# Attention block over 32 batches: projections in f16 parts, probability transposes laid between products, adj copied by ScalarE

## The reference

```python
h = jnp.maximum(_layernorm(x, axis=-1), 0.0)
q = split_heads(h @ Wq.T); k = split_heads(h @ Wk.T); v = split_heads(h @ Wv.T)
a = jnp.einsum('bhnd,bhmd->bhnm', q, k) * scale + (adj + adj)[:, None]
p = softmax of a over the last axis, 0 for a row of a that is all zero
o = einsum('bhnm,bhmd->bhnd', p, v), heads side by side
out = x + o @ Wo.T
```

## Time and profile before

| | us |
|---|---|
| median of 3 runs | 1319.92 (1319.8 to 1320.41) |
| the profiled execution | 1319.87 |
| its span | 1318.1 |
| PE busy | 1288.6 (98% of the span) |
| PE weight loads | 1225.6 (93%) |
| DVE busy | 1130.4 (86%) |
| ACT busy | 1033.8 (78%) |
| POOL busy | 902.1 (68%) |

### The profile page before, as it was taken

One profiled execution on the slowest core, in us unless ns is written; L12 is line 12 of the kernel. 1 busy time (PEld: TensorE's weight loads), 2 busy tenths in 40 slices (PEclk: granted clock), 3 DMA queues, 4 the chain that ended last, 5 costly groups with the idle time before them and its releaser, 6 DMA issues. The chain is left out here.

```text
span 1318.1 us, 43774 instructions
## 1 busy us (share of the span) xinstructions
PE 1288.6 (98%) x13072; PEld 1225.6 (93%) x13072; DVE 1130.4 (86%) x4023; ACT 1033.8 (78%) x2379; POOL 902.1 (68%) x1263
## 2 busy tenths in 40 slices
PE   5899999999999999999999999999999999999996
PEld 5899999999999999999999999999999999999995
DVE  5888888888888888888889888888888888888884
ACT  3788778788787888887888787888788887788874
POOL 5667667667677676676776676776677776676765
PEclk9999999999999999999999999999999999999998
DMA  6445454455354454454454454454544554544441
GB/s 213 104 117 138 108 136 119 115 139 127 109 146 117 109 148 119 112 143 116 114 151 109 122 130 121 123 143 108 131 119 122 133 133 110 139 119 113 126 121 49
DMA packets 90772, 163.88 MB, mean 124 GB/s; under 512 B 14976, under 2 KB 23168, under 8 KB 90752
## 3 DMA queue, kind: packets, MB, share of 16 engines
q1 hardware_dynamic: 90752, 163.64, 47.9%
HBM read 46.14 MB, written 16.78 MB: 48 GB/s over the span
## 5 line engine op out<-in xcount | busy, mean ns | idle before, releaser
L849 POOL TENSOR_TENSOR fold<-minus 128x512 f32<-128x512 f32 x256 | 329.7, 1288 | 325.3 <-DVE bounds L703 325.3
L553 ACT ACTIVATE probs<-minus,bounds 128x256 f32<-128x256 f32 x1024 | 460.2, 500 | 19.1 <-DVE bounds L703 19.1
L564 ACT ACTIVATE pT_hi<-pT_ps 128x512 f16<-128x512 f32 x512 | 306.0, 598 | 154.3 <-PE pT_ps L401 152.6
L721 DVE TENSOR_TENSOR pT_lo<-pT_ps,pT_hi 128x512 f16<-128x512 f32 x512 | 351.1, 686 | 84.5 <-ACT pT_hi L564 84.2
L703 DVE CUSTOM_DVE_ANT_0 minus<-s_ps,adj_now 128x256 f32<-128x256 f32 x1024 | 389.3, 417 | 18.3 <-DVE adj_now L715 14.3
L401 PE MATMUL pT_ps<-ident,probs 128*128 128x128 f32 x2048 | 307.6, 273 | 1.7 <-ACT probs L553 1.6
L328 PE MATMUL job_ps<-hT_hi,w_hi 128*128 128x256 f32 x1024 | 300.4, 293 | 3.1 <-DVE hT_lo L671 2.6
L328 PE MATMUL job_ps<-hT_lo,w_hi 128*128 128x256 f32 x1024 | 290.1, 283 | 0.0
L328 PE MATMUL job_ps<-hT_hi,w_lo 128*128 128x256 f32 x1024 | 289.8, 283 | 0.0
L401 PEld LDWEIGHTS pT_ps<-ident,probs 128*128 128x128 f32 x2048 | 240.4, 140 | 15.4 <-ACT probs L553 2.6
L390 PE MATMUL s_ps<-qk_stack 96*128 96x256 f32 x1024 | 247.1, 323 | 2.2 <-DMA qk_stack<-qk_parts 2.2
(11 more groups left out here) (80 smaller groups left out, 2406.4 us busy)
## 6 DMA issues: line engine op xcount, KB each, us to landing
qk_stack<-qk_parts SPq DMA_DIRECT2D x768, 128.0 KB, 2.3
x_in<-x SPq DMA_DIRECT2D x32, 512.0 KB, 3.4
x_res<-x SPq DMA_DIRECT2D x32, 512.0 KB, 3.6
out<-y SPq DMA_DIRECT2D x64, 256.0 KB, 2.1
adj_in<-adj SPq DMA_DIRECT2D x32, 256.0 KB, 3.6
minus<-wq_t SPq DMA_DIRECT2D x2, 512.0 KB, 6.0
qk_parts<-wv SPq DMA_DIRECT2D x2, 512.0 KB, 10.5
y<-wk_t SPq DMA_DIRECT2D x1, 512.0 KB, 8.4
```

The lines of the kernel that those rows point to most:

```text
L553: end = nc.scalar.activation(probs[hh % 2][:, t, :], minus[hh // 2 % 2][:, hh % 2, t, :], ACT.Exp, bias=bounds[:, hh // 2 % 4, 2 * (hh % 2 ...
L564: nc.scalar.activation(pT_hi[hh % 4][:, :, :], pT_ps[hh % 2][:, :].rearrange("p (m n) -> p m n", m=NT), ACT.Copy).then_inc(pT_high, 1)
L721: nc.vector.tensor_tensor(pT_lo[hh % 4][:, :, :], pT_ps[hh % 2][:, :].rearrange("p (m n) -> p m n", m=NT), pT_hi[hh % 4][:, :, :], ALU.sub ...
L849: nc.gpsimd.tensor_tensor(f1[:, :, :], src[:, :, 0:N // 2], src[:, :, N // 2:N], ALU.add).then_inc(folded1, 1)
```

## The change

Query, key and value products take f16 operands. The three weights come in untransposed, each half is scaled per row by a power of two so that its largest value is near 2^14, transposed on PE, and split in f16; the normalised tokens are multiplied by 2^9. The scales are taken out where the results are read (`q_scale`, `UNTOP`). The output projection stays in float32r.

On PE the units of the step's jobs are laid between the transposes and the scores: T, unit, T, unit, T, unit, T, unit, S, unit, S, unit, then the rest of the units, and V last (before: T, S, V, units). A transpose job now counts 4 units. h1 stands at the start of step 5, ahead of the second half of y0, and is taken at the end of step 5 rather than in step 6. The copy of adj goes from DVE (step 14) to ACT (step 13).

```diff
-PRODUCTS = {"qk": 24, "v": 12, "y": 12, "h": 1, "o": 1}
+PRODUCTS = {"qk": 24, "v": 12, "y": 12, "h": 4, "o": 4}
 JOBS = {
...
-    3: [("v", 3, 0, 3, 12), ("o", 1, -1, 0, 1)],
-    4: [("h", 0, 1, 0, 1), ("y", 0, -1, 0, 6)],
-    5: [("y", 0, -1, 6, 9), ("h", 1, 1, 0, 1), ("y", 0, -1, 9, 12)],
+    3: [("v", 3, 0, 3, 12), ("o", 1, -1, 0, 4)],
+    4: [("h", 0, 1, 0, 4), ("y", 0, -1, 0, 6)],
+    5: [("h", 1, 1, 0, 4), ("y", 0, -1, 6, 12)],
...
+TAKEN_AT_ONCE = ("h", 1)
...
-        w_hi = [sb(f"w_hi{i}", [P, KT, D], F32R) for i in range(4)]
-        w_lo = [sb(f"w_lo{i}", [P, KT, D], F32R) for i in range(4)]
-        WQ, WK, WV, WO = range(4)
+        WQ, WK, WV = range(3)
+        w_hi = [sb(f"w_hi{i}", [P, KT, D], F16) for i in range(3)]
+        w_lo = [sb(f"w_lo{i}", [P, KT, D], F16) for i in range(3)]
+        wo_hi, wo_lo = sb("wo_hi", [P, KT, D], F32R), sb("wo_lo", [P, KT, D], F32R)
...
-        hT_hi = sb("hT_hi", [P, KT, N], F32R)
-        hT_lo = sb("hT_lo", [P, KT, N], F32R)
+        hT_hi = sb("hT_hi", [P, KT, N], F16)
+        hT_lo = sb("hT_lo", [P, KT, N], F16)
...
+            def work(b, hh, first, last, start, stop):
+
+                at = 0
+                for kind, n, d, here, end in jobs_at(hh, first, last):
+                    lo, hi = max(here, here + start - at), min(end, here + stop - at)
+                    if lo < hi:
+                        job(kind, n, d, lo, hi, b)
+                    at += end - here
...
             def body(b, first, last):
                 for hh in range(HEADS):
-                    transpose_probs(b, hh, first and hh < 2)
-                    if hh + AHEAD < HEADS:
-                        scores(b, hh + AHEAD)
-                    elif not last:
-                        scores(b + 1, hh + AHEAD - HEADS)
+                    done = 0
+                    for m in range(NT):
+                        for t in range(NT):
+                            transpose_probs(b, hh, m, t, first and hh < 2)
+                            work(b, hh, first, last, done, done + 1)
+                            done += 1
+                    for t in range(NT):
+                        if hh + AHEAD < HEADS:
+                            scores(b, hh + AHEAD, t)
+                        elif not last:
+                            scores(b + 1, hh + AHEAD - HEADS, t)
+                        work(b, hh, first, last, done, done + 1)
+                        done += 1
+                    work(b, hh, first, last, done, 1000)
 
                     for was in range(hh - 2, hh) if hh % 2 == 0 else ():
                         if was >= 0:
                             values(b, was, first and was < 2)
                         elif not first:
                             values(b - 1, HEADS + was, False)
-                    for kind, n, d, start, stop in jobs_at(hh, first, last):
-                        job(kind, n, d, start, stop, b)
...
                     for kind, n, d in ended_before(hh, first, last):
                         take(kind, n, b + d, first and (kind, d) in (("v", 0), ("qk", 0)))
+                    if hh == HEADS - 3 and not last:
+                        copy_adj(b + 1)
                     high_probs(b, hh, first and hh < 4)
+                    for kind, n, d in ended_in(hh, first, last):
+                        take(kind, n, b + d)
...
+                nc.vector.tensor_reduce(w_scale[:, i, EXTENT, part], w_in[i][:, part, :], AX_X, ALU.max,
+                                        apply_absolute_value=True).then_inc(w_extent, 1)
...
-                        if hh + 2 == HEADS:
-                            copy_adj(b + 1)
                         shift(b + 1, hh + 2 - HEADS, False)
```

More of the change, by code:

```diff
@@ L210, in settled, with weight_waits @@
             engine.sem_inc(went_on[name], 1)
[L212 to L217, removed]
+        def weight_waits(engine, i, half):
+            engine.wait_ge(w_split, TURNS.index((i, half)) + 1)
         def bank(kind, n, b):
@@ L338, in job @@
                 if kind == "h":
-                    if n == 0:
+                    if n == 0 and start == 0:
                         pe.wait_ge(h_ready, b + (d + 1))
[L342 to L345, removed]
+                    for k, t in [divmod(i, NT) for i in range(start, stop)]:
+                        end = nc.tensor.transpose(ps[:, k * N + t * P:k * N + (t + 1) * P],
+                                                  h[:, t, (2 * n + k) * P:(2 * n + k + 1) * P], ident[:, :])
                 elif kind == "qk":
+                    half = PRODUCTS["qk"] // 2
                     if n == 0 and start == 0:
+                        pe.wait_ge(taken["h"], count("h", 0, b + d))
+                    if n == 0 and start <= half // 2 < stop:
                         pe.wait_ge(taken["h"], count("h", 1, b + d))
-                    half = PRODUCTS["qk"] // 2
                     for i, w in enumerate((WQ, WK)):
@@ L361, in job @@
                 elif kind == "o":
[L363 to L367, removed]
+                    if start == 0:
+                        pe.wait_ge(o_ready, (b + d) * PAIRS + 4 * (n + 1))
+                    for k, t in [divmod(i, NT) for i in range(start, stop)]:
+                        end = nc.tensor.transpose(ps[:, k * N + t * P:k * N + (t + 1) * P],
+                                                  o[:, t, (2 * n + k) * P:(2 * n + k + 1) * P], ident[:, :])
                 else:
@@ L482, in _ @@
                 values(B - 1, hh, False)
[L483 removed]
+            job("o", 1, -1, 0, 4, B)
             for n in range(NT):
@@ L647, in low_weight @@
[L647 to L660 removed]
+                at = 3 * TURNS.index((i, half))
@@ new lines, in low_weight @@
+            def low_weight(i, half):
+                at = TURNS.index((i, half))
+                dve.wait_ge(w_high, at + 1)
+                for j in range(2):
+                    cols = slice(half * HALF, (half + 1) * HALF)
+                    end = nc.vector.tensor_tensor(
+                        w_lo[i][:, 2 * j:2 * j + 2, cols],
+                        turn_ps[at % 3][j][:, :].rearrange("p (k n) -> p k n", k=2),
+                        w_hi[i][:, 2 * j:2 * j + 2, cols], ALU.subtract)
```

331 lines of the change are left out of this document (178 added, 153 removed), and 2 rows, old and new, of the table JOBS.

## The result

The changed kernel takes 1550.67 us (median of 4 runs, 1548.86 to 1551.16) against 1319.86 for the kernel before; the ratio is 1.1747, with a 95% interval of 1.1726 to 1.1767. It is slower, as forecast, but by 84 us more than the forecast of 1466 and above the range, which ended at 1530.

A forecast was written before the change was run, and what follows sets the result against it. PE was taken to bound the kernel at 39.8 us a batch. New PE work 35.2, waits 8.5 and clock 0.8 make 44.5 a batch; with 5 us ahead of the loop, 1466 us, range 1390 to 1530.

The forecast's parts named there:

- PE work: PE's products, transposes, S and V in a batch of the new order, without waits: 35.2 us, 4.6 less than 39.8.
- v0 behind y1: Step 14: PE waits 1.2 us for v0's bank, since y1 is taken 3.7 after V of step 12.
- v3 behind qk3: Step 2: PE reaches v3 before DVE, busy in its own order, has taken qk3, and waits 1.7 us.
- o1 behind v2: Step 4: o1 waits 0.7 us for v2, which DVE ends 2.2 us after the V of step 2.
- h0 behind v3: Step 4: h0 waits 1.3 us for v3, which DVE ends about 3.95 us after the V of step 2.
- h1 behind h0: Step 5: h1's bank is free 2.65 us after V, with one T between; PE waits 2.5 us.
- qk0 behind y0: Step 6: y0 ends with step 5 and ACT has other work ahead of it; PE waits 0.8 us.
- qk3 behind v0: Step 0: PE waits 0.3 us at qk3 behind v0.
- clock: Behind the new pauses, some products of y0 and qk0 run at half clock in some batches: 0.8 us a batch.
- the price of T between products: 42 T laid beside f16 products hide their f32 weight load and cost 0.055 us each instead of 0.108.
- Rival 2: Waits come, overlap doesn't: T stays 0.108, f16 products 0.12; 1526 us with the clock, 1500 without; chance 0.14.
- Rival 3: ACT and DVE take earlier jobs in time, so DVE sets the pace: 36.5 us a batch, 1226 us; chance 0.09.

The follow-up runs named there:

- t_f16: The changed kernel with probabilities, identity and the result of T as f16, so the low part of the probabilities is lost; 1468.92 us.
- fast kernel: The changed kernel with PE's order of before and h1 back at its old place, keeping f16 products, scales and adj's copy on ScalarE; 1286.65 us.
- order_f32r: The kernel before with the changed kernel's order on PE, places of taking and adj copy on ScalarE, products still float32r; 1563.10 us.
- grouped_v_last: The changed kernel without the alternation: four T, two S, all units, then V, with h1 at the start of step 5; 1465.32 us.
- v_early: The changed kernel with V right behind the unit after the second S, ahead of the rest of the units; 1435.45 us.
- h1_back: The changed kernel with h1 alone back behind three products of y0 and taken in step 6; 1488.18 us.
- f16_old_adj_dve: The kernel with f16 products and the order of before, with the copy of adj back on DVE ahead of the shift; 1286.92 us.

## Why the prediction failed, step by step

| us a batch | predicted | measured |
|---|---|---|
| PE work | 35.2 | 38.5 |
| v0 behind y1 | 1.2 | 1.1 |
| v3 behind qk3 | 1.7 | 1.4 |
| o1 behind v2 | 0.7 | 0.5 |
| h0 behind v3 | 1.3 | 1.2 |
| h1 behind h0 | 2.5 | 2.5 |
| qk0 behind y0 | 0.8 | 0.8 |
| qk3 behind v0 | 0.3 | 0 |
| waits in all | 8.5 | 7.5 |
| clock | 0.8 | 1.1 |
| batch | 44.5 | 47.05 |

The measured waits are from start to start (h1: 620.82 - 618.18, less the usual 0.11), as means over the batches at full clock; the idle times of the waits view are some 0.2 shorter each, since they begin where a matmul's length ends. The work is 45.98 less the waits.

- **The step that failed is the price of T between products,** the term 42 x 0.055 in the new PE work of 35.2. "I read the 0.108 as the loading of f32 weights" was wrong, and with it 0.055 for such a T: laid between products it cost 0.109, as among transposes. t_f16 puts that price on the 128 f32 data columns. 42 T x 0.054 = 2.3 of the 3.3 that the work was sized too low.
- **With T in f16** a batch at full clock is 43.65, less 8.3 of waits 35.35. That this is about the 35.2 of the sum is chance in part: t_f16 halves all 64 T where the sum halved 42, which is 1.2 less work, and the sum lacks what lies between kinds of work, about as much.
- **The trace of before had a sign of it,** in the mean lengths of its lines view by shape (busy us, mean ns), below. A product of 256 columns is 283 ns long and one of 65 is 192, so one of 128 would be near 222 by an estimate in a straight line between them; T with its 128 f32 columns is 273, and the f16 T of t_f16 is 223. The profile models where a matmul ends, so this is a sign and no proof.

```profile
L401 PE MATMUL pT_ps<-ident,probs 128*128 128x128 f32 x2048 | 307.6, 273 | 1.7 <-ACT probs L553 1.6
L328 PE MATMUL job_ps<-hT_lo,w_hi 128*128 128x256 f32 x1024 | 290.1, 283 | 0.0
L422 PE MATMUL o_ps<-v_parts,pT_hi 128*128 128x65 f16 x2048 | 153.6, 192 | 1.4 <-DVE pT_lo L721 1.0 <-issue 0.2
```

- **The rest of that term is what lies between kinds of work.** The sum of the pieces before was 39.2 of 39.8, as the prediction says itself; after, it took the pieces alone. (Its 16 products for V are right; the 32 of the kernel's description above are not.) The fast kernel shows it too: 144 x 0.109 + 5.6 + 80 x 0.108 + 3.8 + 3.7 is 37.4, and its batch with hardly a wait is 38.63.
- **The f16 product** was right: 0.109 against 0.12.
- **The waits** were right in place, releaser and size, but for qk3's, which didn't come; the sum is 1.0 too high, above all in v3 and qk3. The three chains written out link by link, h1, h0 and v0, came to 0.1, and so did qk0.
- **The clock** was right in its cause and place, and 0.3 low: it falls in 25 of 31 batches, not in half of them, and a fall costs 1.07 x 31 / 25 = 1.3.
- **Outside the loop** 5 was forecast, all of it ahead of the first batch. It was 8.4 there, within the stated bounds of 0 and 12, and 1.9 and 2.7 more came in the first batch and in the last with the end, which the sum had at nothing. Of the 85 us by which the span was missed, 77 lie in the 30 batches of the loop, 3 ahead of it and 5 in those two.
- **Rival 2** had the price of T right. Its work of 39.2 came near the 38.5 by two errors that go against each other: it took the f16 product at 0.12, 144 x 0.011 = 1.6 too much, and left out what lies between kinds of work. It also let v3's and o1's waits shrink by 2.0 where they shrank by 0.5. Its time, 1526, was also the upper end of the range, so that the range held no room for this rival's own errors. Two terms that the forecast called alternatives, all the waits and none of the overlap, came together. The sum of these two was in no rival.
- **Rival 3** didn't come: ACT stood idle for 301.8 us in front of the output copy, with nothing else in its queue that it could do first.

Of the signs named, idle time at h1, h0 and v0, ACT's wait for V and the half-clock stretches came; the pairs at 0.22 instead of 0.165 are the one that was said to prove the forecast wrong.

## What to carry to other kernels

Before laying a short matmul between others to hide its load, find whether its price is load or data: a row in which it stands ahead of cheap work tells it, and here the price of an f32 transpose of 128 columns went with its data. When work is reordered on the engine that sets the pace, count for each buffer what stands between its last use and the next: here 0.57 us of cover less and a chain that starts half a step later cost 8 us in a batch of 39, on engines that were below 90%. Take the parts of a change separately; the f16 products alone, in the old order, were worth 2.5%.

## What the hardware showed that was not expected

- A transpose with 128 f32 data columns takes 0.109 us, an f16 one 0.056; 0.109 is also the price of a product of 256 f16 columns. The Trainium skill, page TensorE: Matmul & The Clock Gate, section Back-to-back issue gap, gives 134 cycles for an isolated matmul of 128 columns and 262 for one of 256. At 2.4 GHz these would be 0.056 and 0.109: the f16 rows agree with it, the f32 transpose needs what it gives for twice its columns. The 81 ns that the same section gives for a sustained pair at 128 columns, on which the prediction's side estimate stood, fit neither row.
- An f32 load of 128 columns has a row of 0.14 us, and its transpose starts 0.056 after the load does. The same page, section LDWEIGHTS (loading the stationary operand), gives columns / 1.2 in ns, 107 for 128. The rows at 634.85 and 634.91 show that a load of about that length or more need not keep starts that far apart.
- PE's idle time ahead of h1, once a batch, and the granted clock of 0.50 behind it: with 2.3 us it fell in 25 of 31 batches (changed kernel) and in 16 of 31 (order_f32r), with 2.4 in 18 of 31 (t_f16), with 1.8 in 12 of 31 (grouped_v_last), with 1.4 in one, the first, ahead of the loop (v_early), and with 1.3 in none (h1_back). So the length of the pause alone doesn't set how often, and what else does is open. Useless work in the pause was worth 33 us.
- The copy of adj took DVE 0.91 in the kernel before and 0.42 in f16_old_adj_dve at the same place in the order. The difference goes with what POOL does at its start. In the loop of the kernel before an operation of POOL was running then (the row below, with the copy at 626.32); it ended 0.63 after the copy's start, and the copy ended 0.28 behind it. In f16_old_adj_dve POOL's operation starts 0.06 behind the copy. In all 33 copies of the two runs that started while POOL was at work, POOL's end came 0.14 to 0.63 after the start and the copy's end 0.28 later. No run varied this alone. No other engine waited for the copy.

```profile
626.21 0.74 POOL L855 TENSOR_TENSOR bounds<-fold 128x256 f32<-128x256 f32 x1
```

```profile
614.86 0.42 DVE L758 COPY adj_now<-adj_in 128x512 f32<-128x512 f32 x1
```

```profile
614.92 0.94 POOL L911 TENSOR_TENSOR bounds<-fold 128x256 f32<-128x256 f32 x1
```
